# Attention output kept with its dimensions on partitions, its row sums inverted by chunk and spread through DRAM

## The reference, cut

```python
x = x + 0.5 * ffn(layernorm(x))      # base linear + top-2 of 8 LoRA experts
x = x + attn(layernorm(x))
x = x + 0.5 * ffn(layernorm(x))
# attn: q, k, v by linears with sign weights, one scale per output; 32 heads of 16, 8 kv heads
scores = einsum('bhqd,bhkd->bhqk', q, k) / 4
out    = einsum('bhqk,bhkd->bhqd', softmax(scores), v)
y      = linear(out as [token, head*16], sign(o_weight)) * o_scale;  nan_to_num(y)
```

## Time and profile before

| | |
|---|---|
| median of 3 runs | 1157.1 us (1156.59 to 1159.24) |
| the profiled execution | 1159.3 us, of which its span is 1157.5 us |
| mean TensorE clock granted | 0.967 of full speed |
| busy | PE 93%, DVE 73%, ACT 63%, POOL 25% |
| DMA | 59.42 MB in 87359 packets, of which 44144 under 512 bytes |
| instructions | 16340 |

### The profile page before, as it was taken

One profiled execution on the slowest core, in us unless ns is written; L12 is line 12 of the kernel. 1 busy time (PEld: TensorE's weight loads), 2 busy tenths in 40 slices (PEclk: granted clock), 3 DMA queues, 4 the chain that ended last, 5 costly groups with the idle time before them and its releaser, 6 DMA issues.

```text
span 1157.5 us, 16340 instructions
## 1 busy us (share of the span) xinstructions
PE 1076.3 (93%) x5968; PEld 484.5 (42%) x5968; DVE 844.4 (73%) x1146; ACT 727.1 (63%) x1361; POOL 293.3 (25%) x485
## 2 busy tenths in 40 slices
PE   5989887999999999999999999999999999998857
PEld 3778661344334433344334333433343334333436
DVE  5766679767776778877888678777977887782173
ACT  6457432757865787675776567666766675768420
POOL 5365556302510250410140014003200320041010
PEclk9989886999999999999999999999999999999979
DMA  7122331021210113011210121031002001300300
GB/s 254 38 90 88 101 103 49 28 65 26 61 34 32 30 53 83 27 32 38 68 27 26 53 54 26 26 81 27 26 26 80 27 27 26 81 6 7 90 1 36
DMA packets 87359, 59.42 MB, mean 51 GB/s; under 512 B 44144, under 2 KB 73328, under 8 KB 87280
## 3 DMA queue, kind: packets, MB, share of 16 engines
q1 hardware_dynamic: 87280, 58.39, 17.6%
HBM read 37.64 MB, written 20.32 MB: 50 GB/s over the span
## 4 chain that ended last, share of the span: by engine, by line
PE 74%; DVE 12%; ACT 6%; POOL 3%; issue 3%; DMA 1%; SPq 1%; DVEq 0%; POOLq 0%
PE ps_out L1452 20%; PE ps_score L1440 18%; PE ps_max L1415 16%; PE ps_fill L1373 5%; DVE neg_max L1218 3%; ACT probs L954 3%; PE ps_fill L1400 2%; PE ps_fill L1341 1%; PE ps_fill L1355 1%; PE ps_fill L1377 1%; DVE neg_max L1043 1%; DVE zd L1110 1%; PE ps_out L1373 1%; PE ps_max L1429 1%; PE ps_fill L1347 1%
## 5 line engine op out<-in xcount | busy, mean ns | idle before, releaser
L954 ACT ACTIVATE probs<-ps_score 128x512 f32<-128x512 f32 x992 | 539.0, 597 | 272.5 <-PE ps_score L1440 270.8
L1218 DVE TENSOR_REDUCE neg_max<-ps_max 128x1 f32<-128x1024 f32 x480 | 572.1, 1220 | 168.6 <-PE ps_max L1415 167.0
L1415 PE MATMUL ps_max<-kst,qst 96*128 96x512 bf16 x1024 | 294.0, 388 | 14.6 <-DVE neg_max L1043 5.7
L1440 PE MATMUL ps_score<-qst,kst 99*128 99x512 bf16 x992 | 305.1, 385 | 1.2 <-ACT probs L954 0.8
L1452 PE MATMUL ps_out<-probs,v_ring 128*32 128x512 f32 x2048 | 273.6, 606 | 8.1 <-ACT o_sb L960 5.3
L1440 PEld LDWEIGHTS ps_score<-qst,kst 99*128 99x128 bf16 x992 | 77.8, 97 | 254.3 <-ACT probs L954 210.0
L1415 PEld LDWEIGHTS ps_max<-kst,qst 96*128 96x128 bf16 x1024 | 88.4, 98 | 143.3 <-issue 17.6
L793 POOL CAST shift<-neg_max 128x16 bf16<-128x16 f32 x32 | 7.5, 236 | 463.3 <-DVE neg_max L1218 458.9
L1452 PEld LDWEIGHTS ps_out<-probs,v_ring 128*32 128x32 f32 x2048 | 41.0, 108 | 101.9 <-issue 92.0
L889 ACT ACTIVATE xn<-xc,ln_shift,rstd 128x512 f32<-128x512 f32 x48 | 38.5, 811 | 30.0 <-POOL ln_shift L690 19.0
L1373 PE MATMUL ps_fill<-wb_h,xt_h 128*128 128x512 f32 x84 | 46.9, 559 | 1.6 <-DVE xc L1205 0.8
(11 more groups left out here) (254 smaller groups left out, 1331.8 us busy)
## 6 DMA issues: line engine op xcount, KB each, us to landing
qst<-q_dram SPq DMA_DIRECT2D x192, 64.0 KB, 2.2
q_dram<-zm SPq DMA_DIRECT2D x24, 256.0 KB, 2.6
kst<-k_dram SPq DMA_DIRECT2D x192, 32.0 KB, 2.2
xc<-x SPq DMA_DIRECT2D x8, 512.0 KB, 3.8
x_dram<-xc SPq DMA_DIRECT2D x8, 512.0 KB, 2.8
xc<-x_dram SPq DMA_DIRECT2D x8, 512.0 KB, 4.2
out<-xc SPq DMA_DIRECT2D x8, 512.0 KB, 3.2
att_dram<-att SPq DMA_DIRECT2D x31, 128.0 KB, 2.2
```

The costliest lines, as they stand in the source:

```text
L954: act.activation(probs[:, kt % 2, j, :], score_bank(i, uu, j), ACT.Exp, scale=1.0 / HD ** 0.5).then_inc(probs_ready, 1)
L1218: dve.tensor_reduce(neg_max[:, uu % 2, t:t + 1], ps_max[max_slot(uu, pos)][:, :, :], AXY, ALU.max, negate=True).then_inc(max_read, 1)
L1415: last = pe.matmul(ps_max[slot][:, half, :], qst[0:SR, r, j, q * P:(q + 1) * P], kst[0:SR, r, half * 512:half * 512 + 512], start=True, st ...
L1440: pe.matmul(score_bank(i, uu, j), kst[0:SR + PARTS, uu, kt * P:(kt + 1) * P], qst[0:SR + PARTS, uu, j, :], start=True, stop=True).then_inc ...
```

## The change

The output is never turned. ScalarE's copy `o_sb` is stored as it is, dimensions and sums on partitions, 256 KB per unit, as soon as it is ready. A back chunk loads 512 rows of output straight into `att_t` (the memory of `xn`), with four DMAs, and its sums as 32 heads by 256 tokens, laid out as 128 partitions by 64 columns (`sums`). VectorE inverts these (NR), SP stores them to `recip_dram` and loads them back with each row repeated 16 times (NL), so that `recip_t` (the memory of `zd`) fits `att_t`. VectorE multiplies (N0a, N0b), ScalarE rounds into `xt_h`, VectorE subtracts into `xt_l` (N0al, N0bl). The matmuls of Oa and Ob stay, and have a wait on the rest. In the tail, the sums of the first 28 heads are inverted after the last body; the last unit's rows come from `o_sb` by 16 DMAs (`load_last_out`), and their sums are inverted after the spreading, 64 partitions by 256 columns. The plans of SP and VectorE in the bodies do what the diff shows; lines with "..." are left out.

```diff
-    12 * [""] + ["T0a", "T0al", "", "T0b", "T0bl", "", "Oa0", "Oa1", "C0", "Ob0", "Ob1", "", "G0 C1", "P0", "", "G1", "P1",
+    10 * [""] + ["NR", "", "NL", "", "N0a", "N0al N0b", "N0bl", "", "Oa0", "Oa1", "C0", "Ob0", "Ob1", "", "G0 C1", "P0", "", "G1", "P1",
...
-        att_dram = nc.dram_tensor("att_dram", [T // P, KV, P, REP * HD], F32, kind="Internal").ap()
+        att_dram = nc.dram_tensor("att_dram", [T // BLK, KV, P, BLK], F32, kind="Internal").ap()
...
+                if pos == "NR":
+                    store_recip(ch)
+                if pos == "NL":
+                    load_recip(ch)
...
-                heads = KV - 1 if ch.tail else KV
-                for t in range(CT):
-                    sp.dma_start(xn[s][:, t, 0:heads * REP * HD].rearrange("p (k d) -> p k d", k=heads),
-                                 att_dram[bass.ds(a * 2 + t, 1), 0:heads, :, :].rearrange("o k p d -> p (o k) d")
-                                 ).then_inc(chunk_loaded[s], 16)
+                heads = att_dram[bass.ds(a // 2, 1), :, :, (a % 2) * CH:(a % 2) * CH + CH].rearrange(
+                    "o k (j x) t -> (o k j) x t", x=2 * HD)
+                known = H - REP if ch.tail else H
+                groups = P // H
+                sp.dma_start(sums[s][0:known * groups, :],
+                             heads[0:known, HD, :].rearrange("h (g t) -> h g t", g=groups)).then_inc(sums_loaded[s], 16)
+                for c in range(DC):
+                    h0, h1 = c * (P // HD), min((c + 1) * (P // HD), known)
+                    sp.dma_start(att_t[s][0:(h1 - h0) * HD, c, :], heads[h0:h1, 0:HD, :]).then_inc(chunk_loaded[s], 16)
...
+            def store_recip(ch):
+
+                s, n = ch.slot, ch.n
+                a = n if not ch.tail else NCH - 2 + s
+                known = H - REP if ch.tail else H
+                groups = P // H
+                sp.wait_ge(recip_ready[s], n + 1)
+                sp.dma_start(recip_dram[a, 0:known, :].rearrange("h (g t) -> h g t", g=groups),
+                             sums[s][0:known * groups, :]).then_inc(recip_stored[s], 16)
+
+            def load_recip(ch):
+
+                s, n = ch.slot, ch.n
+                a = n if not ch.tail else NCH - 2 + s
+                known = H - REP if ch.tail else H
+                sp.wait_ge(recip_stored[s], (n + 1) * 16)
+                for c in range(DC):
+                    h0, h1 = c * (P // HD), min((c + 1) * (P // HD), known)
+                    sp.dma_start(recip_t[s][0:(h1 - h0) * HD, c, :],
+                                 recip_dram[a, h0:h1, :].unsqueeze(1).broadcast_to([h1 - h0, HD, CH])
+                                 ).then_inc(recip_loaded[s], 16)
+
+            def load_last_out(ch):
+
+                s = ch.slot
+                sp.wait_ge(o_copied, NU)
+                for j in range(REP):
+                    to = slice(((KV - 1) % 2 * REP + j) * HD, ((KV - 1) % 2 * REP + j + 1) * HD)
+                    for dst, r0 in ((att_t[s], 32 * j), (recip_t[s], 32 * j + HD)):
+                        sp.dma_start(dst[to, DC - 1, :], o_sb[r0:r0 + HD, (NU - 1) % 2, s * CH:s * CH + CH]
+                                     ).then_inc(last_out_loaded[s], 16)
...
-                if isinstance(i, int) and UB * i + uu < 2:
-                    sp.wait_ge(max_read, use + 1)
-                else:
-                    sp.wait_ge(rows_copied, i * UB + (uu - 1))
...
-            def store_att(i, uu, use):
+            def store_att(i, uu):
 
                 j = i + uu // UB
-                sp.wait_ge(max_read, use + 1)
-                sp.dma_start(att_dram[bass.ds((j // 2) * QT, QT), bass.ds((j % 2) * UB + uu % UB, 1), :, :]
-                             .rearrange("q o p d -> p q (o d)"), att[:, uu % 2, :, :]).then_inc(att_stored[uu % 2], 16)
+                sp.wait_ge(o_copied, i * UB + (uu + 1))
+                sp.dma_start(att_dram[bass.ds(j // 2, 1), bass.ds((j % 2) * UB + uu % UB, 1), :, :]
+                             .rearrange("o k p t -> (o k p) t"), o_sb[:, uu % 2, :]).then_inc(att_stored[uu % 2], 16)
...
-                    if kt == 4 and not (first and uu == 0):
-                        store_att(i, uu - 1, turn_use(i, uu, last))
-                    if slot == 5 and load_next is not None:
+                    if kt == 1 and not (first and uu == 0):
+                        store_att(i, uu - 1)
+                    if slot == 4 and load_next is not None:
...
+                        for ch in tail:
+                            store_recip(ch)
+                        for ch in tail:
+                            load_recip(ch)
...
+            for ch in tail:
+                load_last_out(ch)
...
+                if pos in ("N0a", "N0b"):
+                    t = 0 if pos.endswith("a") else 1
+                    act.wait_ge(att_normed[s], n * 2 + (t + 1))
+                    act.activation(xt_h[s][:, :, t * P:(t + 1) * P], att_t[s][:, :, t * P:(t + 1) * P],
+                                   ACT.Copy).then_inc(xt_h_ready[s], 1)
...
+                unit = UB * i + uu
+                if unit >= 2:
+                    act.wait_ge(att_stored[unit % 2], 16 * (unit // 2))
...
+            def invert_sums(ch):
+
+                s, n = ch.slot, ch.n
+                known = H - REP if ch.tail else H
+                dve.wait_ge(sums_loaded[s], (n + 1) * 16)
+                dve.reciprocal(sums[s][0:known * (P // H), :], sums[s][0:known * (P // H), :]).then_inc(recip_ready[s], 1)
...
+                if pos == "NR":
+                    invert_sums(ch)
+                if pos in ("N0a", "N0b"):
+                    t = 0 if pos == "N0a" else 1
+                    tok = slice(t * P, (t + 1) * P)
+                    dve.wait_ge(chunk_loaded[s], ch.load)
+                    dve.wait_ge(recip_loaded[s], (n + 1) * 16 * DC)
+                    if ch.tail and t == 0:
+                        late = slice((KV - 1) % 2 * REP * HD, P)
+                        dve.wait_ge(last_out_loaded[s], 16 * 2 * REP)
+                        dve.reciprocal(recip_t[s][late, DC - 1, :], recip_t[s][late, DC - 1, :]).then_inc(last_recip_ready[s], 1)
+                        dve.wait_ge(last_recip_ready[s], 1)
+                    dve.tensor_tensor(att_t[s][:, :, tok], att_t[s][:, :, tok], recip_t[s][:, :, tok],
+                                      ALU.mult).then_inc(att_normed[s], 1)
+                if pos in ("N0al", "N0bl"):
+                    t = 0 if pos == "N0al" else 1
+                    tok = slice(t * P, (t + 1) * P)
+                    dve.wait_ge(xt_h_ready[s], ch.t0 + (t + 1))
+                    dve.tensor_tensor(xt_l[s][:, :, tok], att_t[s][:, :, tok], xt_h[s][:, :, tok].bitcast(F32),
+                                      ALU.subtract).then_inc(att_low_ready[s], 1)
...
                         use, at = turn_use(i, uu, last), turn_slot(uu, last)
                         if not (last and uu == 3):
-                            copy_rows(i, uu + 1, use, at, max_read if first and uu == 0 else rows_copied)
-                        if not (first and uu == 0):
-                            normalise(i, uu - 1, use, at)
+                            copy_rows(i, uu + 1, use, at)
...
-            normalise(8, -1, max_use(7, 2, 2), max_slot(2, 2))
+            for ch in (Chunk("back", 0, 6, tail=True), Chunk("back", 1, 0, tail=True)):
+                invert_sums(ch)
...
                 if pos in ("Oa", "Ob"):
+                    if piece == 0:
+                        pe.wait_ge(att_low_ready[s], ch.n * 2 + (t + 1))
...
                 max_slot_free(use)
-                if rows:
-                    pe.wait_ge(shift_parts, i * (4 * UB) + 4 * (uu + 2))
-                    last = pe.transpose(ps_max[slot][:, 0, 0:P // 2].bitcast(BF16), shift[:, (uu + 1) % 2, :], identb[:, :])
-                if out:
-                    pe.wait_ge(o_copied, i * UB + uu)
-                    for q in range(QT):
-                        last = pe.transpose(ps_max[slot][:, 1, q * P:(q + 1) * P], o_sb[:, (uu - 1) % 2, q * P:(q + 1) * P],
-                                            ident[:, :])
-                last.then_inc(max_scores, 1)
+                pe.wait_ge(shift_parts, i * (4 * UB) + 4 * (uu + 2))
+                pe.transpose(ps_max[slot][:, 0, 0:P // 2].bitcast(BF16), shift[:, (uu + 1) % 2, :],
+                             identb[:, :]).then_inc(max_scores, 1)
...
-            turn(8, 0, max_use(7, 2, 2), max_slot(2, 2), rows=False)
```

More of the change, by code:

```diff
@@ L191, in tn @@
     def tn(self, stage):
-        return ["T1a", "T1b", "T2a", "T2b"].index(stage) if self.front else ["T0a", "T0b", "T1a", "T1b"].index(stage)
+        return ["T1a", "T1b", "T2a", "T2b"].index(stage) if self.front else ["N0a", "N0b", "T1a", "T1b"].index(stage)
 def alone_order(text):
@@ L274, in macaron @@
         zd = [sb(f"zd{s}", [P, ZW], F32) for s in range(2)]
+        sums = [sb(f"sums{s}", [P, CH * H // P], F32) for s in range(2)]
```

(27 more changed lines are left out.)

46 lines of the change are left out of this document (16 added, 30 removed).

## The result

The changed kernel takes 1192.6 us (median of 4 runs, 1192.0 to 1197.8), the kernel before, beside it on the same chip, 1158.2 us (1156.6 to 1160.7): a ratio of 1.031, with an interval of 1.027 to 1.034. Slower was the right sign. +34 us against a forecast of +9 was not, and the time lies over 10 us beyond 1182, the upper end of the range.

What follows compares the result with a forecast made beforehand. TensorE was taken to set the pace in attention, with one chain through all engines at the end. The terms -18.6 + 16 + 11 = +8.4 gave 1166 us, range 1148 to 1182.

Steps and rivals of the forecast that it cites:

- What bounds the kernel: Attention bodies: TensorE sets the pace, busy for 93% of the span, VectorE a small way behind.
- Part 1: Attention bodies: removing 31 turns of the output gives back 0.6 us each, -18.6 us (-13 to -27).
- Part 2: Six chunks in the bodies: the new chain between engines costs 2.6 us net each, +16 us (-5 to +32).
- lands, at 2.2 us like a `kst` load, at 566.9: Chunk chain: the fourth replicated load of reciprocals starts at 564.7 and lands 2.2 us later.
- so it waits 0.5: Chunk chain: VectorE's first multiply, N0a, reached at 566.4, waits 0.5 us for the replicated reciprocals.
- The far bound: Chunk chain: replicated loads could take 4.9 us to land, like the old load of `att_dram`.
- the queue order: Chunk: the fixed order of steps in the engines' queues, without the 0.5 us for data, costs 2.9 us.
- Part 3: Tail: SP's queued stores and loads and the late inversions delay projection and guard, +11 us (+7 to +16).
- The reciprocal: VectorE's inversions: 0.49 us for 64 columns in a chunk, 1.5 us for 256 in the tail.
- the slope: VectorE's reciprocals: 5.2 ns a column, from 166 and 239 ns for 2 and 16 columns.
- rival 2: Chunks: broadcast loads land after 4.9 us, N0a ends 2.7 us later six times, +16, 1182 us; chance 0.13.
- Rival 1: Chunks: the chain is covered at ScalarE's wait at N0a, part 2 is -5, 1141 us; chance 0.22.

Runs made afterwards that it cites:

- moved_turn: `moved` with the four transposes of the output and their wait put back into each turn on TensorE, read by nobody: 1168.2 us, 1.008.
- no_trip: The changed kernel without the reciprocals' inversion and DRAM round trip in bodies 2 to 7, multiplying by a constant tile instead: 1172.2 us, 1.011.
- moved: The changed kernel with the chunk's inversion and loads one slot earlier and ScalarE's roundings one slot behind their multiplies: 1160.5 us, 1.002.
- k16: The changed kernel with reciprocals stored twice, so each replicated load's slowest dimension is 16 instead of 8: 1192.5 us, 1.028.
- keep: The changed kernel with 14 extra matmuls, read by nobody, where TensorE would stand still in slot 8 of bodies 2 to 7: 1187.0 us, 1.024.

## Why the prediction was right in sign and wrong in size

- **What bounds the kernel:** right. Where ScalarE's probabilities came late, TensorE stood still, and the kernel grew.
- **Part 1, the turn, -18.6:** right, 31 × 0.57 = -17.7. Only some 0.25 of the 0.57 is TensorE's transposes (moved_turn). The 0.42 us of weight loads was therefore no price of TensorE's part, and VectorE's part, by subtraction, is the larger one; that it would be hidden was too strict.
- **Part 2, the chunk: the step that failed is "lands, at 2.2 us like a `kst` load, at 566.9", and with it "so it waits 0.5".** The last replicated load was used 4.7 us after its issue, and the multiply waited 2.2 us on average, 2.66 in the chunk shown. A `kst` load was the wrong row to compare with. The far bound, 4.9 us, was near the truth for the landing, but it was never asked what else SP has in flight at that time. The term is 3.4 gross in the forecast and 6.7 measured. Of these, 2.7 are the queue order (no_trip's bodies at the upper clock; forecast 2.9). 2.6 are the late data, for which the forecast had 0.5: the unit with the stall takes 28.5 us on average over the five bodies, and 25.9 in no_trip. The last 1.4 are the lower clock in the unit behind it (28.7 us on average, not 27.3), for which the forecast had nothing.
- **Why the loads land late:** the Trainium skill, "DMA: Bandwidth & Descriptors", section "Why a DMA increments its semaphore by 16 and not by 1", has the number of DMA engines follow from the slowest dimension, here 8 heads. The traces agree with it: in `moved`, where nothing else runs beside the loads, the share of the engines is 0.50 and 0.49 (the windows below), and in k16 it goes up to 0.61. In `moved` SP's next issue comes at least 1.8 us after that of the last load (0.6 in the changed kernel), and the last one lands 3.0 to 3.2 us after its issue in all six chunks, against the 2.2 of the forecast. So about 0.9 us of the lateness is the load's own. The rest comes with the Q and K loads issued right behind it: with them the changed kernel's last load lands after 4.0 to 4.6 us, in five chunks. The sixth stands in the last body, which loads no Q and K, and there it lands after 3.2 us and the multiply waits 1.23 us (the rows below).

```profile
556.00:557.00 1.00, 1.00 (x6) 0.29 (x3) 0.73 (x1) 0.79 (x3) 0.00 (x0) 1.00 0.50 177
557.00:558.00 1.00, 1.00 (x9) 0.16 (x8) 1.00 (x2) 1.00 (x2) 0.00 (x0) 1.00 0.49 170
```
```profile
1024.24 2.46 SPq L560 DMA_DIRECT2D zd<-recip_dram  x4
...
1029.39 0.69 DVE L1243 TENSOR_TENSOR xn<-xn,zd 128x512 f32<-128x512 f32 x1 [1.23 <-DMA zd<-recip_dram]
```

- **The clock was left out.** The prediction considered a slow start only for the tail. The stalls of 2.5 to 4.1 us were followed by its lower level in every chunk. Behind the shorter ones of no_trip (1.15 us, then 0.59) it fell in two of six, and only there the next unit took 28.4 to 28.7 us instead of 27.3. keep shows the price, 5.6 us over the kernel with the fall gone from five chunks of six.
- **Part 3, the tail, +11:** +13.5, inside its bounds. SP's issues of the replicated loads are 0.61 us apart and those of `o_sb` rows 0.63, not 0.47; a late inversion takes 1.75 us, not 1.5. The first projection matmul comes 18.6 us after VectorE's last body step, where 15.8 was forecast. Sixteen such issues stand before the row that the first late inversion needs: 16 × 0.15 = 2.4, less 0.7 for stores that land in 1.5 us instead of 2.2; with 0.25 for the inversion that is 1.9 of the 2.7. The rest is small gaps that I didn't follow.
- **The reciprocal:** 544 ns for 64 columns and 1750 for 256, against the 490 and 1490 of the slope: 6.3 ns a column between them, not 5.2. The Trainium skill, "VectorE: DVE Perf Modes", section "Walkthrough: the 8-slice pipeline in each mode", read as 8 cycles a column, would have given some 0.7 and 2.3 us, an estimate; the rows lie nearer the slope.
- **The rivals:** rival 2, late broadcast loads, is the mechanism that came true, and its time of 1182 was 10 short, from the clock and the tail. It had 0.13; the half share of DMA engines was there to be counted in the diff, and deserved more. Rival 1 fell: ScalarE did reach its rounding before VectorE's multiply, even without the trip. Rival 3 fell as a price, with the 0.57, though its picture is partly right: TensorE's transposes cost nothing in half of the units, and VectorE's release is the larger part.

Summed over the span: the forecast was +8.4 and the profile shows +33.0. Of the 24.6 between them the late data and the clock are 6 × 4.0 = 24, less the 3 that the forecast had for the data (6 × 0.5), the queue order 6 × -0.2 = -1, the turn 0.9, the tail 2.5, and 2.1 stood already before the first output copy. These make 25.5, which closes within the rounding of single profiles. no_trip, which takes away the late data in all six chunks and the lower clock in four, took back 20.4 us of the first item's 24.

## What to carry to other kernels

A result that goes out to DRAM and comes back to several engines should be given room for its slowest load, counted by how many DMA engines can carry it, how long its issues stand in the queue and what is issued right behind. When a chain hops between engines whose queues are fixed by slot, place each consumer a slot behind its producer, not in the same slot. The two together, with the same instructions, were worth 32 us here; how they share it wasn't measured. At the end of a kernel, issue what doesn't depend on the last step before it, so that only the last step's data is left to move.

## What the runs showed of the hardware that was not expected

- SP's issues are not all 0.47 us apart: replicated loads 0.61, loads of 16 partitions out of `o_sb` 0.63.
- The 32 KB store of the reciprocals landed 1.4 us after its issue in the changed kernel (median), the 128 KB stores of the earlier trace rows in 2.2. In `moved`, where the same store stands nearer behind the loads of the attention output, it took 1.4 to 2.9, median 2.2.
- Four replicated loads of 128 KB, issued 0.6 us apart: the last lands 3.0 to 3.2 us after its issue with nothing issued for 1.8 us or more behind it (`moved`), and 4.0 to 4.6 with the loads of Q and K right behind (the changed kernel).
- After a stand-still of 3.9 us in the middle of dense work the clock was at its lower level for some 6 us of work. Stand-stills of 1.15 us and, shortly behind, 0.59 us were followed by 3.4 us at the lower level in two chunks of six (no_trip). Keeping TensorE at work with matmuls that nobody reads made the kernel 5.6 us faster.
- Splitting the replicated loads over 16 instead of 8 rows of DRAM raised their height from 177 GB/s (`moved`) to 209 (k16), and the time from first issue to use fell by 1.5 us.
